# A third factor buffer and packed convolution taps, with the product of delta and x on GpSimd and that of x and D on ScalarE

## The chip, the cores and the metric

The kernel runs on one core of a Trainium2 chip. The time is that of the whole launch in microseconds of the device, as the median of several runs. The profile is of one further execution, whose own time is given beside its span (the time from its first to its last instruction). Engines are named as in the profile: PE (matmuls), DVE (VectorE), ACT (ScalarE), POOL (GpSimd), SP (the queue that issues the DMAs).

## What is computed

Two stages over x of shape (2, 2048, 512), with a residual after each. The first, in which all edits lie, is a small gated recurrence of 64 channels, whose result y0 is expanded to 512 by Wo, and then a Mamba block on it. Cut to what matters:

```python
# recurrence of 64 channels ("cond"): y0 = c_t * state;  h = y0 @ Wo + bo
xn = layernorm(h) * ln_g + ln_b
x_br, z = split(xn @ W_in, 2)                  # 1024 channels each
xb = silu(causal_conv4(x_br, conv_w) + conv_b) # depthwise, 4 taps
Bm, Cm = xb @ W_b, xb @ W_c                    # 16 states
delta = softplus(xb @ W_delta + b_delta)
A_bar = exp(delta[..., None] * A)              # (time, channel, state)
Bx = delta[..., None] * Bm[:, :, None, :] * xb[..., None]
h_t = A_bar_t * h_(t-1) + Bx_t                 # scan over time
y = sum_state(h * Cm) + xb * Dp
x = x + ((y * silu(z)) @ W_out + h)
# second stage: low-rank layer and a feed-forward with weights cut to -1, 0, 1 and activations to 8 bits
```

## The kernel before

All arithmetic of the first stage is in fp32. Time is cut into 16 blocks of T = 256 steps (8 of each of the two sequences, in turn). Channels lie on the 128 partitions, in ND = 8 tiles `dt`; the 16 states are cut into NG = 4 groups of G = 4. A step of the inner loop is a pair (tile, group), q = 0 to NQ - 1 = 31, and every engine walks through the same 32 of them in each block, in an order written out by hand:

- ACT makes the factors A_bar of a group: 4 exponentials of 128x255 from `delta` (line 702), written to one of two PSUM buffers `a_ps` of 4 banks in all. It may start on a buffer once the scan two groups back is through (line 699).
- DVE makes Bx of the next group, one 128x1024 instruction that multiplies u = delta * x (held over the 4 states) by `Bbc`, the broadcast rows of B in SBUF (line 856, `bx`); it writes into a slot of the SBUF `ring` of four. Then it scans the present group (line 864, `scans`), in place in the ring, with the factors as first input and the ring slot as second. Column 0 of each state carries the state over from the last block, so that one scan covers four states.
- For every second tile DVE first makes u for a pair of tiles, from `delta` and `xb`, both in SBUF, into the PSUM bank `u_ps` (line 835).
- POOL copies the last column of the states (line 465) and multiplies the ring slot by `Cbc` in two halves of 128x512 (line 472), both in SBUF. Once for each tile it makes `xdp` = x * D, 128x256 (line 459).
- PE turns and sums the products in the bank `yT_ps` (line 1069, `turn_states`), with `xdp` as first term (line 1063). A ring slot is free for line 856 once its turns are done.
- DVE gates the turned sum with silu(z) (line 799).

Between these steps each engine does the work of the next block (`front`) and what is left of the last (`back`): projections, the small recurrence, the convolution as matmuls, silu, B and C, delta in two halves (the softplus ends on POOL, line 423), and the product with W_out. `plan`, `next_plan` and `back_plan` say at which q. The banks `work[0]` and `work[1]` are handed out in a fixed order of jobs (`BANK`, `jobs_before`). The convolution and its projection are one product: `Mx` holds four matrices of 66 rows (64 channels, one for the bias, one for ln_b), one for each tap, and `x` (lines 1000 to 1011) sums four matmuls of the shifted rows `y0s`. `y0back` (line 535) fills `y0s` on ACT. PSUM is full: 4 banks of factors, 2 of work, one each for `yT_ps` and `u_ps`.

`big[0]`, 128 x 8192 fp32 in SBUF, holds W_in at first, then Mx, Mz, Wcen, the kept y0 and small pieces; in the last block SP fills it with the first feed-forward weights in eight pieces of 1024 columns (lines 306 to 311), among stores of small rows. The second stage waits for all eight (line 1236).

```python
dve.tensor_tensor(u_ps[:, :, 1:T], delta[:, par, dt:dt + 2, 1:T], xb[:, par, dt:dt + 2, 1:T], ALU.mult)
dve.tensor_tensor(ring[:, q % RING, :, :], u_ps[:, dt % 2:dt % 2 + 1, :].to_broadcast([P, G, T]),
                  Bbc[:, G * g:G * g + G, :], ALU.mult)
```

## Time and profile before

| | |
|---|---|
| Time, median of 3 runs | 2658.17 us (2652.7 to 2659.58) |
| Profiled execution: its time and its span | 2653.91 us, 2651.9 us |
| Busy over the span: PE, DVE, ACT, POOL | 2309.5, 2265.5, 1669.0, 1728.4 us |
| Mean granted clock of PE | 0.95 of full speed |
| Line 472 on POOL, Cbc products | 1283.1 us in 1024 |
| Line 864 on DVE, scans | 1168.0 us in 512 |
| Line 856 on DVE, B times u | 619.7 us in 512 |
| Line 702 on ACT, factors | 852.9 us in 2048 |

Busy time is the time in which an engine has an instruction of the program in work; "idle before" is what it stood still ahead of a group, put down to the engine that released it last. In the profile an instruction counts as busy from its start on also while it is held up inside the engine.

### The profile page before, as it was taken

The numbers are of one execution on the slowest core, as the hardware profiler recorded it, in microseconds if no ns is written. First come the engines' busy times: TensorE is split into PE (matmuls) and PEld (weight loads), VectorE is DVE, ScalarE is ACT, GpSimd is POOL, SyncE is SP. The second block draws the span as 40 slices with busy tenths as digits, with TensorE's granted clock in tenths as the row PEclk, the third lists the DMA queues.
The fourth block names the chain that finished last, engine by engine and source line by source line (L and its number), as shares of the span: only waits on it lengthen the run. The fifth ranks groups of instructions, "written<-read, shape, count | busy, mean of one in ns | idle before, by whom it ended". The sixth has DMA issues, their size and how long they took to land. (4 is left out here: it accounts for less than half of the span.)

```text
span 2651.9 us, 34212 instructions
## 1 busy us (share of the span) xinstructions
PE 2309.5 (87%) x11520; PEld 1586.2 (60%) x11520; DVE 2265.5 (85%) x2232; ACT 1669.0 (63%) x3332; POOL 1728.4 (65%) x2042
## 2 busy tenths in 40 slices
PE   7778889888898988888988888888888875999997
PEld 5566667676666666757666666666666322444443
DVE  2399999999999999899999999999999835888886
ACT  2567676667667676767676767676766534555554
POOL 0278787878787878778787778787878711222221
PEclk8889999999999999999999999999998987999999
DMA  4102020202010110102020202020104621111110
GB/s 186 72 1 72 9 76 6 76 5 80 16 65 21 61 53 28 65 17 73 9 72 10 72 10 72 10 76 5 72 10 189 233 83 56 60 64 66 59 52 24
DMA packets 48299, 151.74 MB, mean 57 GB/s; under 512 B 8069, under 2 KB 8965, under 8 KB 45198
## 3 DMA queue, kind: packets, MB, share of 16 engines
q1 hardware_dynamic: 48142, 149.76, 15.9%
q8 instruction: 84, 1.38, 0.2%
q14 instruction: 73, 0.60, 0.1%
HBM read 132.37 MB, written 17.37 MB: 56 GB/s over the span
## 5 line engine op out<-in xcount | busy, mean ns | idle before, releaser
L472 POOL TENSOR_TENSOR ring<-ring,Cbc 128x512 f32<-128x512 f32 x1024 | 1283.1, 1275 | 44.5 <-POOL carry L465 0.4
L864 DVE TENSOR_TENSOR_SCAN ring<-a_ps,ring 128x1024 f32<-128x1024 f32 x512 | 1168.0, 2281 | 106.7 <-ACT a_ps L702 105.2
L702 ACT ACTIVATE a_ps<-delta,nA 128x255 f32<-128x255 f32 x2048 | 852.9, 468 | 380.3 <-DVE ring L864 379.4
L1069 PE MATMUL yT_ps<-ident,ring 128*128 128x128 f32 x4096 | 588.1, 284 | 163.5 <-POOL ring L472 160.0
L1069 PEld LDWEIGHTS yT_ps<-ident,ring 128*128 128x128 f32 x4096 | 475.0, 145 | 282.2 <-POOL ring L472 241.9
L856 DVE TENSOR_TENSOR ring<-u_ps,Bbc 128x1024 f32<-128x1024 f32 x512 | 619.7, 1210 | 16.0 <-PE yT_ps L1069 9.3
L1035 PE MATMUL work<-xb,big 128*128 128x256 f32 x2048 | 476.8, 385 | 10.1 <-ACT zs L560 10.1
L1035 PEld LDWEIGHTS work<-xb,big 128*128 128x128 f32 x2048 | 385.5, 193 | 79.5 <-issue 16.9
L465 POOL TENSOR_TENSOR carry<-ring,half 128x4 f32<-128x4 f32 x512 | 127.1, 248 | 361.2 <-DVE ring L864 359.7
L1051 PE MATMUL work<-Wout,xb 128*128 128x512 f32 x512 | 237.7, 599 | 0.0
L1414 POOL TENSOR_TENSOR m<-m,pows 128x1 f32<-128x1 f32 x64 | 34.2, 549 | 311.4 <-DVE m L1546 311.4
L1008 PE MATMUL work<-y0s,big 128*128 128x256 f32 x1024 | 234.7, 380 | 0.7 <-issue 0.7
L1008 PEld LDWEIGHTS work<-y0s,big 128*128 128x128 f32 x1024 | 188.6, 190 | 24.6 <-issue 1.0
L1051 PEld LDWEIGHTS work<-Wout,xb 128*128 128x128 f32 x512 | 98.1, 196 | 116.4 <-issue 116.4
L1481 PE MATMUL o_ps<-q,qhT 128*128 128x512 bf16 x512 | 119.3, 387 | 11.8 <-DVE qhT L1579 11.8
L1445 PE MATMUL x_ps<-lay,x2T 128*128 128x512 f32 x256 | 122.0, 621 | 0.7 <-ACT x2T L1506 0.7
L567 ACT ACTIVATE xb<-work,V 128x256 f32<-128x256 f32 x128 | 53.5, 469 | 103.7 <-PE work L1008 103.7
L1460 PE MATMUL h_ps<-q,qaT 128*128 128x512 bf16 x512 | 115.7, 379 | 0.0
L423 POOL TENSOR_TENSOR delta<-delta,lnbuf 128x1024 f32<-128x1024 f32 x32 | 75.6, 2363 | 58.8 <-ACT lnbuf L616 58.8
L1024 PE MATMUL work<-xb,Wbc 128*32 128x256 f32 x256 | 77.4, 471 | 33.1 <-ACT xb L576 33.1
L1512 ACT ACTIVATE hb<-hb 128x2048 f32<-128x2048 f32 x32 | 61.2, 1912 | 65.7 <-DVE hb L1565 65.7
L1565 DVE SCALAR_TENSOR_TENSOR hb<-h_ps,m,b1r 128x2048 f32<-128x2048 f32 x32 | 75.2, 2350 | 27.8 <-PE h_ps L1460 27.8
(197 smaller groups left out, 2508.1 us busy)
## 6 DMA issues: line engine op xcount, KB each, us to landing
Bbc<-bc_rows SPq DMA_DIRECT2D x64, 512.0 KB, 4.6
Cbc<-bc_rows SPq DMA_DIRECT2D x64, 512.0 KB, 3.7
xT<-in_xT SPq DMA_DIRECT2D x16, 514.0 KB, 3.5
x_rows<-x2row SPq DMA_DIRECT2D x32, 256.0 KB, 2.0
xp<-x_rows SPq DMA_DIRECT2D x32, 256.0 KB, 2.7
xx<-in_x SPq DMA_DIRECT2D x32, 256.0 KB, 3.0
out_rows<-orow SPq DMA_DIRECT2D x32, 256.0 KB, 2.0
delta<-in_c_w SPq DMA_DIRECT2D x6, 1024.0 KB, 5.3
```

The costliest lines, as they stand in the source:

```text
L465: nc.gpsimd.tensor_tensor(carry[:, par, dt, G * g:G * g + G].rearrange("p (g o) -> p g o", o=1), h[:, :, T - 1:T], ident1, ALU.mult).then_ ...
L472: nc.gpsimd.tensor_tensor(hp, hp, Cbc[:, G * g + GP * c:G * g + GP * c + GP, :], ALU.mult)\
L702: r = nc.scalar.activation(a_ps[q % 2][:, i, 1:T], delta[:, par, dt, 1:T], ACT.Exp, scale=nA[:, dt, s:s + 1])
L856: dve.tensor_tensor(ring[:, q % RING, :, :], u_ps[:, dt % 2:dt % 2 + 1, :].to_broadcast([P, G, T]), Bbc[:, G * g:G * g + G, :], ALU.mult). ...
L864: dve.tensor_tensor_scan(ring[:, q % RING, :, :].rearrange("p g t -> p (g t)"), a_ps[q % 2][:, :, :].rearrange("p g t -> p (g t)"), ring[: ...
L1008: r = pe.matmul(ps[:, T * m:T * m + T], Mx[:, tap, c:c + P], y0s[:, fp, tap:tap + T], start=(tap == 0), stop=(tap == 3))
L1035: r = pe.matmul(ps[:, T * m:T * m + T], Wd[:, d, c:c + P], xb[:, fp, d, :], start=(d == 0), stop=(d == ND - 1))
L1051: r = pe.matmul(ps[:, :], xb[:, fp, d, P * tt:P * tt + P], Wout[:, d, :], start=False, stop=(d == ND - 1))
L1069: r = pe.matmul(yT_ps[:, tt, :], ring[:, q % RING, i, P * tt:P * tt + P], ident[:, :], is_transpose=True, start=False, stop=(g == NG - 1 a ...
L1445: r = pe.matmul(x3_ps[:, :], x2T[:, d, :], lay[:, batch, d, :], start=(d == 0), stop=(d == KD - 1))
L1460: r = pe.matmul(h_ps[:, 512 * c:512 * c + 512], qaT[:, d, :], q1[:, d, 512 * c:512 * c + 512], start=(d == 0), stop=(d == KD - 1))
L1481: r = pe.matmul(o_ps[:, :], qhT[:, d, :], q2[:, d, :], start=(d == 0), stop=(d == KF - 1))
```

## The change

- A third factor buffer `a_sb` in SBUF (in `big[0]`); group number n of the whole run uses buffer n mod 3, on ACT and on DVE, and ACT may be three groups ahead.
- u is made by POOL (`inputs`), a pair of tiles ahead, into two buffers in `big[0]` (SBUF); the bank `u_ps` is given up. DVE's line 856 waits for POOL's product and reads u from there.
- `xdp` is made by ACT (`skip`) and no more by POOL.
- Taps: the rows for taps 0 and 1 of the 64 channels are packed one above the other into one matrix of 128 rows, read against `yp`, that ACT copies together from `y0s`; the two further rows of taps 0 and 1 go to partitions 96 and 97 of the matrices for taps 2 and 3, and `y0s` has shifted copies there. So 3 matmuls of 128 rows stand for 4 of 66. ACT makes three more small copies a block. The setup is changed to match.
- The pieces of `big[0]` that hold these buffers till later (3, 7 and 6) are loaded later: piece 3 once line 856 has come to its last 8 groups, piece 7 after its last, piece 6 after the last scan.

The diff, without the declarations and the setup of Mx:

```diff
...
-        Mx = big[0][:, 0:4 * DI].rearrange("p (k c) -> p k c", k=4)
+        Mx = big[0][:, 0:3 * DI].rearrange("p (k c) -> p k c", k=3)
+        yp = big[0][:, 3 * DI:3 * DI + T]
         Mz = big[0][:, 4 * DI:5 * DI]
-        y0k = big[0][:, 6 * DI:6 * DI + 2 * T].rearrange("p (b t) -> p b t", b=2)
+        y0k = big[0][:, 5 * DI + D:6 * DI].rearrange("p (b t) -> p b t", b=2)
+        a_sb = big[0][:, 6 * DI:7 * DI].rearrange("p (g t) -> p g t", g=G)
...
+        a_of = [a_ps[0], a_ps[1], a_sb]
+        NA = len(a_of)
         abank = [a_ps[i // 2][:, 2 * (i % 2):2 * (i % 2) + 2, :].rearrange("p a b -> p (a b)") for i in range(4)]
-        u_full = pb("u_ps", [P, 512])
-        u_ps = u_full[:, :].rearrange("p (m t) -> p m t", m=2)
+        u_of = [big[0][:, c:c + 2 * T].rearrange("p (m t) -> p m t", m=2) for c in (3 * DI + T, 7 * DI + D)]
...
-                        if 2 <= c < 9:
+                        if 2 <= c < 8 and c != 5:
                             sp.dma_start(big[0][:, DI * (c - 2):DI * (c - 1)], f_w1[:, DI * (c - 2):DI * (c - 1)])\
                                 .then_inc(s_big[0], 16)
-                    sp.wait_ge(s_col0, NCOL * NBLK)
+                    sp.wait_ge(s_bx, NQ * NBLK - 8)
+                    sp.dma_start(big[0][:, 3 * DI:4 * DI], f_w1[:, 3 * DI:4 * DI]).then_inc(s_big[0], 16)
+                    sp.wait_ge(s_bx, NQ * NBLK)
                     sp.dma_start(big[0][:, 7 * DI:8 * DI], f_w1[:, 7 * DI:8 * DI]).then_inc(s_big[0], 16)
+                    sp.wait_ge(s_scan, NQ * NBLK)
+                    sp.dma_start(big[0][:, 6 * DI:7 * DI], f_w1[:, 6 * DI:7 * DI]).then_inc(s_big[0], 16)
...
+            def inputs(b, bp, j):
+                pool.wait_ge(s_delta, 2 * b + j // 2 + 1)
+                pool.wait_ge(s_xb, 2 * b + j // 2 + 1)
+                wait(pool, s_bx, NQ * b + 8 * (j - 1))
+                nc.gpsimd.tensor_tensor(u_of[j % 2][:, :, 1:T], delta[:, bp, 2 * j:2 * j + 2, 1:T],
+                                        xb[:, bp, 2 * j:2 * j + 2, 1:T], ALU.mult).then_inc(s_u, 1)
             def step(k, par, front, back, scan):
                 for q in range(NQ):
                     dt, g = q // NG, q % NG
+                    if front and q == SUMS[0] + 1:
+                        if isinstance(k, int) and k == -1:
+                            pool.wait_ge(s_mz, 2)
+                        inputs(k + 1, 1 - par, 0)
+                    if scan and q in (3, 11, 19):
+                        inputs(k, par, (q + 5) // 8)
...
-                    if g == 0:
-
-                        wait(pool, s_xb, 2 * k + (2 if dt >= ND // 2 else 1))
-                        wait(pool, s_tr, NQ * k + NG * (dt - 2) + 1)
-                        nc.gpsimd.tensor_tensor(xdp[:, dt % 2, :], xb[:, par, dt, :],
-                                                V[:, V_DP + dt:V_DP + dt + 1].to_broadcast([P, T]), ALU.mult)\
-                            .then_inc(s_xdp, 1)
-
...
-                    act.wait_ge(s_yh, n + 1)
-                    nc.scalar.activation(y0s[0:NY, fp, 3:T + 3], ps[0:NY, 0:T], ACT.Copy).then_inc(free[BANK["YB"]], 1)
+                    act.wait_ge(s_yh, 2 * n + 1)
+                    nc.scalar.activation(y0s[0:NY, fp, 3:T + 3], ps[0:NY, 0:T], ACT.Copy).then_inc(s_yh, 1)
+                    act.wait_ge(s_yh, 2 * n + 2)
+                    nc.scalar.activation(yp[0:N0, :], y0s[0:N0, fp, 0:T], ACT.Copy)
+                    nc.scalar.activation(yp[N0:2 * N0, :], y0s[0:N0, fp, 1:T + 1], ACT.Copy)
+                    nc.scalar.activation(y0s[CROW:CROW + 2, fp, 2:T + 3], y0s[N0:NY, fp, 0:T + 1], ACT.Copy)\
+                        .then_inc(free[BANK["YB"]], 1)
...
+                def skip(b, bp, dt):
+                    wait(act, s_xb, 2 * b + (2 if dt >= ND // 2 else 1))
+                    wait(act, s_tr, NQ * b + NG * (dt - 2) + 1)
+                    nc.scalar.activation(xdp[:, dt % 2, :], xb[:, bp, dt, :], ACT.Copy, scale=V[:, V_DP + dt:V_DP + dt + 1])\
+                        .then_inc(s_xdp, 1)
...
+                    if scan and g == 3 and dt < ND - 1:
+                        skip(k, par, dt + 1)
+                    if front and q == NQ - 3:
+                        skip(n, fp, 0)
...
-                    wait(act, s_scan, NQ * k + q - 1)
+                        act.wait_ge(s_aclr, 5)
+                    wait(act, s_scan, NQ * k + q - NA + 1)
                     for i in range(G):
                         s = G * g + i
-                        r = nc.scalar.activation(a_ps[q % 2][:, i, 1:T], delta[:, par, dt, 1:T], ACT.Exp,
+                        r = nc.scalar.activation(a_of[(NQ * k + q) % NA][:, i, 1:T], delta[:, par, dt, 1:T], ACT.Exp,
...
                 def mx_scale():
+                    dve.wait_ge(s_mtz, 1)
                     for m in range(ND):
                         if m % 4 == 0:
                             dve.wait_ge(s_mxt, m // 4 + 1)
                         ps = abank[m // 4][:, NY * (m % 4):NY * (m % 4) + NY]
-                        for tap in range(4):
-                            r = dve.tensor_scalar(MTk[:, m, tap, :], ps, V[:, V_CW + 4 * m + tap:V_CW + 4 * m + tap + 1],
-                                                  None, ALU.mult)
+                        cw = [V[:, V_CW + 4 * m + tap:V_CW + 4 * m + tap + 1] for tap in range(4)]
+                        for tap in range(2):
+                            dve.tensor_scalar(MTk[:, m, 0, N0 * tap:N0 * tap + N0], ps[:, 0:N0], cw[tap], None, ALU.mult)
+                            dve.tensor_scalar(MTk[:, m, 1 + tap, CROW:CROW + 2], ps[:, N0:NY], cw[tap], None, ALU.mult)
+                            r = dve.tensor_scalar(MTk[:, m, 1 + tap, 0:NY], ps, cw[2 + tap], None, ALU.mult)
                         r.then_inc(s_mxs, 1)
...
-                        delta_ready(dve, k, dt)
-                        dve.wait_ge(s_xb, 2 * k + (2 if dt >= ND // 2 else 1))
-                        wait(dve, s_bx, NQ * k + q)
-                        dve.tensor_tensor(u_ps[:, :, 1:T], delta[:, par, dt:dt + 2, 1:T], xb[:, par, dt:dt + 2, 1:T],
-                                          ALU.mult).then_inc(s_u, 1)
                         if isinstance(k, int) and k == 0:
-                            dve.wait_ge(s_aclr, 1)
+                            dve.wait_ge(s_aclr, 2)
                         dve.wait_ge(s_u, ND // 2 * k + dt // 2 + 1)
...
                     dve.tensor_tensor(ring[:, q % RING, :, :],
-                                      u_ps[:, dt % 2:dt % 2 + 1, :].to_broadcast([P, G, T]),
+                                      u_of[dt // 2 % 2][:, dt % 2:dt % 2 + 1, :].to_broadcast([P, G, T]),
                                       Bbc[:, G * g:G * g + G, :], ALU.mult).then_inc(s_bx, 1)
...
                     dve.tensor_tensor_scan(ring[:, q % RING, :, :].rearrange("p g t -> p (g t)"),
-                                           a_ps[q % 2][:, :, :].rearrange("p g t -> p (g t)"),
+                                           a_of[(NQ * k + q) % NA][:, :, :].rearrange("p g t -> p (g t)"),
                                            ring[:, q % RING, :, :].rearrange("p g t -> p (g t)"), 0.0,
                                            ALU.mult, ALU.add).then_inc(s_scan, 1)
...
-                    for tap in range(4):
-                        r = pe.matmul(ps[:, T * m:T * m + T], Mx[:, tap, c:c + P], y0s[:, fp, tap:tap + T],
-                                      start=(tap == 0), stop=(tap == 3))
+                    for i, rows in enumerate((yp[:, :], y0s[:, fp, 2:T + 2], y0s[:, fp, 3:T + 3])):
+                        r = pe.matmul(ps[:, T * m:T * m + T], Mx[:, i, c:c + P], rows, start=(i == 0), stop=(i == 2))
...
```

## Rows read from the trace of the kernel before

**Rows 1.** Stretches, three of sixteen blocks: us, then busy time by engine, clock, DMA.

```profile
core 0: us, PE busy (x) PEld busy (x) DVE busy (x) ACT busy (x) POOL busy (x), PEclk, DMA share, GB/s
97.90:234.00 136.10, 111.16 (x560) 88.66 (x560) 115.79 (x94) 92.01 (x200) 97.17 (x120) 0.89 0.06 20
...
1242.90:1369.10 126.20, 111.97 (x573) 83.78 (x572) 117.96 (x96) 85.72 (x190) 100.51 (x119) 0.96 0.12 43
...
2000.30:2130.00 129.70, 115.01 (x508) 58.84 (x506) 120.02 (x97) 71.73 (x160) 98.90 (x115) 0.95 0.60 222
```

**Rows 2.** Waits of the whole run: us in total, times, longest.

```profile
ACT a_ps L702 <- DVE ring L864: 379.4, 300, 4.1
POOL carry L465 <- DVE ring L864: 359.7, 323, 5.3
...
DVE ring L864 <- ACT a_ps L702: 105.2, 63, 4.6
...
DVE ring L856 <- PE yT_ps L1069: 9.3, 17, 2.9
```

**Rows 3.** Groups by line: busy us, mean ns of one, idle before.

```profile
L472 POOL TENSOR_TENSOR ring<-ring,Cbc 128x512 f32<-128x512 f32 x1024 | 1283.1, 1275 | 44.5 <-POOL carry L465 0.4
L864 DVE TENSOR_TENSOR_SCAN ring<-a_ps,ring 128x1024 f32<-128x1024 f32 x512 | 1168.0, 2281 | 106.7 <-ACT a_ps L702 105.2
...
L856 DVE TENSOR_TENSOR ring<-u_ps,Bbc 128x1024 f32<-128x1024 f32 x512 | 619.7, 1210 | 16.0 <-PE yT_ps L1069 9.3
...
L1008 PE MATMUL work<-y0s,big 128*128 128x256 f32 x1024 | 234.7, 380 | 0.7 <-issue 0.7
...
L459 POOL TENSOR_TENSOR xdp<-xb,V 128x256 f32<-128x256 f32 x128 | 79.1, 618 | 0.1
...
L835 DVE TENSOR_TENSOR u_ps<-delta,xb 128x510 f32<-128x510 f32 x64 | 58.3, 911 | 46.6 <-POOL delta L423 46.6
L567 ACT ACTIVATE xb<-work,V 128x256 f32<-128x256 f32 x128 | 53.5, 469 | 103.7 <-PE work L1008 103.7
...
L540 ACT ACTIVATE y0s<-work 66x256 f32<-66x256 f32 x16 | 6.1, 382 | 0.5
```

**Rows 4.** Lines one by one: durations in ns min/median/max, first and last start.

```profile
L835 DVE TENSOR_TENSOR u_ps<-delta,xb x64: 666/675/1774, 98.0 to 2096.6; 128x510 f32<-128x510 f32 x64
...
L472 POOL TENSOR_TENSOR ring<-ring,Cbc x1024: 1255/1274/1782, 105.5 to 2131.9; 128x512 f32<-128x512 f32 x171
...
L465 POOL TENSOR_TENSOR carry<-ring,half x512: 192/202/659, 105.2 to 2130.4; 128x4 f32<-128x4 f32 x171
...
L864 DVE TENSOR_TENSOR_SCAN ring<-a_ps,ring x512: 2266/2280/2292, 102.8 to 2127.5; 128x1024 f32<-128x1024 f32 x171
...
L856 DVE TENSOR_TENSOR ring<-u_ps,Bbc x512: 1191/1202/1226, 100.4 to 2124.1; 128x1024 f32<-128x1024 f32 x171
```

**Rows 5.** Timeline at 1242 us: start, duration, engine, line.

```profile
1242.53 2.50 POOL L472 TENSOR_TENSOR ring<-ring,Cbc 128x512 f32<-128x512 f32 x2
...
1243.82 1.77 DVE L835 TENSOR_TENSOR u_ps<-delta,xb 128x510 f32<-128x510 f32 x1
...
1244.99 0.64 POOL L465 TENSOR_TENSOR carry<-ring,half 128x4 f32<-128x4 f32 x1
```

**Rows 6.** Timeline at 1210 us, the same product with POOL idle.

```profile
1210.16 0.68 DVE L835 TENSOR_TENSOR u_ps<-delta,xb 128x510 f32<-128x510 f32 x1
1210.33 0.56 POOL L465 TENSOR_TENSOR carry<-ring,half 128x4 f32<-128x4 f32 x1 [0.52 <-DVE ring L864]
```

**Rows 7.** Timeline at 739 us, the product started ahead of POOL's second.

```profile
738.88 2.95 POOL L472 TENSOR_TENSOR ring<-ring,Cbc 128x512 f32<-128x512 f32 x2
...
740.03 0.67 DVE L835 TENSOR_TENSOR u_ps<-delta,xb 128x510 f32<-128x510 f32 x1
```

**Rows 8.** DMA issues: KB each, median us to landing.

```profile
big<-in_f_w SPq DMA_DIRECT2D x8, 512.0 KB, 6.4
```

**Rows 9.** The reading of the feed-forward weights, line 1237.

```profile
L1237 ACT ACTIVATE q<-big x2: 7015/7024/7032, 2162.2 to 2169.3; 128x8192 bf16<-128x8192 f32 x2
```

More of the change, by code:

```diff
@@ L33 @@
 NY = N0 + 2
+CROW = 96
 EPS = 1e-5
@@ L156, in scan_phase @@
         WoTg = xdp[:, :, :].rearrange("p a b -> p (a b)")[:, 0:KD * NY].rearrange("p (d n) -> p d n", d=KD)
-        MTk = ring[:, 1:RING, :, :].rearrange("p a b c -> p (a b c)")[:, 0:ND * 4 * NY]\
-            .rearrange("p (m k n) -> p m k n", m=ND, k=4)
+        MTk = ring[:, 1:RING, :, :].rearrange("p a b c -> p (a b c)")[:, 0:ND * 3 * P]\
+            .rearrange("p (m k n) -> p m k n", m=ND, k=3)
         cond = V[:, V_COND:V_COND + 2 * KD].rearrange("p (d b) -> p d b", b=2)
@@ L194, in scan_phase @@
         s_mxs = sem("s_mxs")
+        s_mtz = sem("s_mtz")
         s_mxp = sem("s_mxp")
@@ L550, in mx_copy @@
                         act.wait_ge(s_mxp, m + 1)
-                        nc.scalar.activation(Mx[0:NY, :, P * m:P * m + P],
-                                             abank[2 + m % 2][0:NY, :].rearrange("p (k c) -> p k c", k=4), ACT.Copy)\
+                        nc.scalar.activation(Mx[:, :, P * m:P * m + P],
+                                             abank[2 + m % 2][:, 0:3 * P].rearrange("p (k c) -> p k c", k=3), ACT.Copy)\
                             .then_inc(s_mxc, 1)
@@ L697, in step @@
                         act.wait_ge(s_setD, 8)
-                        act.wait_ge(s_aclr, 3)
-                    wait(act, s_scan, NQ * k + q - 1)
+                        act.wait_ge(s_aclr, 5)
+                    wait(act, s_scan, NQ * k + q - NA + 1)
                     for i in range(G):
                         s = G * g + i
-                        r = nc.scalar.activation(a_ps[q % 2][:, i, 1:T], delta[:, par, dt, 1:T], ACT.Exp,
+                        r = nc.scalar.activation(a_of[(NQ * k + q) % NA][:, i, 1:T], delta[:, par, dt, 1:T], ACT.Exp,
                                                  scale=nA[:, dt, s:s + 1])
@@ L723, in _ @@
             dve.tensor_scalar(nA[:, :, :], nA[:, :, :], -1.0, None, ALU.mult).then_inc(s_setD, 1)
+            dve.memset(MTk[:, :, 1:3, NY:P], 0.0).then_inc(s_mtz, 1)
             dve.wait_ge(s_w[0], 16)
@@ L850, in bx @@
                     elif g == 0:
-                        if dt % 2:
-                            dve.wait_ge(s_bx, NQ * k + q)
+                        dve.wait_ge(s_bx, NQ * k + q)
                         dve.tensor_reduce(Bbc[:, :, 0], first[:, dt, :].rearrange("p (s o) -> p s o", o=1), AX.X, ALU.add)\
@@ L877, in step @@
                             .then_inc(s_wcen, 1)
-                        dve.memset(u_ps[:, :, 0:1], 1.0).then_inc(s_aclr, 1)
+                        for i in range(2):
+                            dve.memset(u_of[i][:, :, 0:1], 1.0).then_inc(s_aclr, 1)
+                        dve.memset(a_sb[:, :, 0:1], 0.0).then_inc(s_aclr, 1)
                         dve.wait_ge(s_mxc, ND)
@@ L995, in turn_m @@
                             pe.wait_ge(s_mxc, m - 1)
-                        for tap in range(4):
-                            r = pe.transpose(abank[2 + m % 2][0:NY, P * tap:P * tap + P], MTk[:, m, tap, :], ident[:, :])
+                        for i in range(3):
+                            r = pe.transpose(abank[2 + m % 2][:, P * i:P * i + P], MTk[:, m, i, :], ident[:, :])
                         r.then_inc(s_mxp, 1)
@@ L1006, in x @@
                     c = P * (2 * j + m)
-                    for tap in range(4):
-                        r = pe.matmul(ps[:, T * m:T * m + T], Mx[:, tap, c:c + P], y0s[:, fp, tap:tap + T],
-                                      start=(tap == 0), stop=(tap == 3))
+                    for i, rows in enumerate((yp[:, :], y0s[:, fp, 2:T + 2], y0s[:, fp, 3:T + 3])):
+                        r = pe.matmul(ps[:, T * m:T * m + T], Mx[:, i, c:c + P], rows, start=(i == 0), stop=(i == 2))
                     if m:
@@ L1015, in z @@
                     tt, c = j // 2, 512 * (j % 2)
-                    pe.matmul(ps[:, :], y0s[:, fp, 3 + P * tt:3 + P * tt + P], Mz[:, c:c + 512],
+                    pe.matmul(ps[:, :], y0s[0:NY, fp, 3 + P * tt:3 + P * tt + P], Mz[0:NY, c:c + 512],
                               start=True, stop=True).then_inc(full[BANK[f"Z{j}"]], 1)
```

## The prediction

> **What bounds the kernel now.** I read the page first for busy shares and slices, then the stretches of one block each, then the waits, then the durations of the groups. The scan phase runs from 98 to about 2130 us; the rest is the feed-forward phase, which no edit reaches except through three loads. The phase is periodic: a block takes 126.2 us, in which DVE is busy 118.0, PE 111.9, POOL 100.5 and ACT 85.7 [rows 1]. DVE is the bound: it is idle for 8.2 us a block, and most of that is the scan waiting for ACT's factors, 105.2 us in 63 waits, 6.6 a block [rows 2]. ACT may run only two groups ahead, and what else it has to do between two groups comes through to DVE. ACT and POOL wait for the scan far more than it waits for them [rows 2], so they have room: 40 and 26 us a block.
>
> Then I asked why the product of delta and x on DVE has a mean of 911 ns and a median of 675 [rows 3, 4]. The timeline answers. At 1243.82 the product starts while POOL's pair of Cbc products, begun at 1242.53, still runs; it takes 1.77 us and ends at 1245.59, 0.56 after POOL's pair has ended at 1245.03 [rows 5]. At 1210.16 POOL is idle as it starts; now it takes 0.68, and POOL's small copy, begun 0.17 later, takes 0.56 in place of its usual 0.20 and ends just after it [rows 4, 6]. At 740.03 the product starts a little before POOL's second Cbc product: it takes 0.67, and POOL's pair 2.95 in place of 2.50 [rows 5, 7]. So these two engines exclude each other for a whole instruction, whoever came first going first. The product is the one frequent DVE instruction here whose two inputs both lie in SBUF. The B-times-u product (line 856) takes u from PSUM, the scan (864) its factors from PSUM, and both keep to their durations beside a POOL that is busy four fifths of the time: 1191 to 1226 and 2266 to 2292 ns [rows 3, 4]. The two PSUM operands keep DVE and POOL apart.
>
> **What the change does to this.** It moves u to SBUF, and with it every one of the 512 instructions of line 856 gets two SBUF inputs; and it puts the third factor buffer in SBUF, so that every third scan does too. The exclusion now concerns 64 short products; it will concern 512 + 171 long instructions, against a POOL that all the while multiplies by Cbc from SBUF.
>
> The Trainium skill has the same thing as a rule: "SBUF — State Buffer", section "Who interferes with whom", says that a DVE instruction with two SBUF inputs contends with a GpSimd instruction that reads SBUF, that the one issued first has the shared port pair for the whole instruction, and that the other blocks fully. By that rule this trace agrees (1.77 for 0.68 us). The page does not name the scan; with the rule applied to it the sum is the one below, without it that of the second rival.
>
> **The sum, per block.** What must be laid end to end is POOL's own work plus what DVE holds POOL out.
> - POOL now: 100.5 [rows 1]. Less 8 products of x and D at 0.618: 4.9. Plus 4 products of delta and x; the nearest row is the Cbc product, 512 elements with two SBUF inputs, 1283.1 / 1024 = 1.25 each: 5.0 [rows 3]. Less what DVE's old product cost it, three times 0.36 and once 0.45 a block, 1.5 [rows 4, 6, 7]. Together 99.1.
> - Each exclusive instruction of DVE: of one that waited, 0.56 of 0.68 came after POOL's end, so 0.12 of it is hidden behind POOL. The small copy behind it ended 0.44 late where DVE needed 0.56 [rows 5], so POOL hides 0.12 too. An exclusive instruction costs POOL its duration less 0.24.
> - Line 856: 32 x (1.20 - 0.24) = 30.7. Scans on the SBUF buffer: 171 / 16 = 10.7 a block x (2.28 - 0.24) = 21.8. The durations are those of PSUM operands [rows 3, 4]; the product with SBUF alone, 675 ns for 510 elements, lies on the same line (1202 - 675 = 527 ns for 514 more), so I don't change them.
> - 99.1 + 30.7 + 21.8 = 151.6.
>
> Does DVE come out longer? Its own work is 118.0 - 58.3 / 16 = 114.3 [rows 1, 3]. A scan on SBUF stands right behind line 856 and right ahead of the next, so one POOL instruction slips in on each side: 10.7 x 2 x (1.25 - 0.12) = 24. The other 21.3 of line 856 meet POOL at a random place, some 0.5 each: 11. That is 149, a little less: POOL ends last, but closely, so the ring of four states won't always keep POOL fed. For that idle time I add an estimate of 3 (between 0 and the 8.2 that the bound engine is idle today). 154.6 a block, 28.4 more than 126.2; over 16 blocks (the first and last are about as long as the others [rows 1]) 454 us. The profiled execution took 2653.9 us for a span of 2651.9, and the median of the runs is 2658.2, 4 us above; on 2654 the sum gives **3108 us**.
>
> Bounds of this case: without idle time 151.6, so 3060; with both engines' full durations and nothing hidden, 99.1 + 38.4 + 24.3 = 161.8, so 3224.
>
> **The parts that cost nothing**, and what covers them:
> - *Products of x and D on ACT*: 8 a block at about 0.47, that of a 128x256 copy of line 567 [rows 3], 3.8 us, in ACT's idle 40 us. ACT issues the product for a tile ahead of waiting factors, and the state that it waits for was turned a tile before. Without the cover: 3.8 x 16 = 60 us.
> - *Third factor buffer*: worth at most the 6.6 us a block of waits for factors, 105 us in all, if DVE stayed the bound. Here it is not: DVE waits for POOL instead, ACT is early anyway, and the gain is nothing.
> - *u made by POOL ahead*: takes 3.6 us a block from DVE (58.3 in all) and adds the 5.0 counted above. Queued behind it on POOL are the copy of the states and the Cbc products; behind these PE's turns and so DVE's next line 856. The wait of POOL on delta and x is met long before; the one on line 856 eight groups back too. At a block's start DVE waits for a product that POOL issues three groups ahead of the end.
> - *Packed taps*: 3 matmuls in place of 4, a quarter of the 234.7 us of PE in line 1008, 3.7 a block [rows 3]. PE is at 112 of 126 now and would be at 108 of 155. Three more small ACT copies (0.38 each, row of line 540 [rows 3]) lie ahead of the first of them and hold up PE's queue by some 1.1 us a block, 18 in all if nothing covered it; PE's 46 idle us do.
> - *Loads of the feed-forward weights*: pieces 3, 7 and 6 now wait on SP for DVE's last instructions, and three small row stores stand behind them. The last piece starts at the end of the last scan, about 2130 us on the old scale, lands 6.4 us later, and is read at 2162 [rows 4, 8, 9]. Hidden; without it 6 us once.
> - *Setup* ahead of the first block: 48 smaller DVE multiplications for 32, 24 turns for 32, and one memset. A few us of either sign, once.
>
> **Rivals.**
> 1. *The exclusion does not touch line 856 or the scan* (a held broadcast, or a scan that reads at half pace, might leave POOL room). Then DVE falls to 114.3 and, with two thirds of the factor waits gone, idles some 2: 116.3, 9.9 less a block, 158 in all: **2496 us**. Against it: the row of line 835 is the same operation on the same engine; only held u and the output's place differ. It decides if line 856 keeps 1.20 us beside a busy POOL. 5 in 100.
> 2. *Only line 856 excludes, the scan doesn't*: 99.1 + 30.7 + 3 = 132.8, 6.6 more, **2760 us**. For it: no row shows a scan with two SBUF inputs, and it takes an element in two of the product's times. 10 in 100.
> 3. *The exclusion costs more than the hidden 0.24 allows*: each hand-over at full price and DVE and POOL both starving each other through the ring. 161.8 + 3 = 164.8, **3272 us**. 7 in 100.
> 4. *Gains and losses cancel within 0.3%*: needs an exclusion of a tenth of the size seen. 1 in 100.
>
> The forecast's own case has 77 in 100, and 3050 to 3230 around it. The range from 2740 to 3240 leaves out rivals 1 and 3 and the lower half of 2. A difference under 0.3% can't be told from no change; faster 0.05, same 0.01, slower 0.94.
>
> **What would show it.** Right: line 856 with a mean far over 1.20 us, split between about 1.2 and 2.3; a third of the scans well above 2.28, the others at it; the Cbc product with a mean over 1.6 for 1.27; POOL's share of the scan phase near 100% by the profile's count; waits of the scan for factors almost gone, those of line 856 for PE's turns (9.3 us now [rows 2]) grown to hundreds; a block of about 155 us. Wrong: line 856 at 1.20 flat (rival 1), or all scans at 2.28 (rival 2). The mechanism would also be mis-sized if DVE could take the port twice in a row, past a waiting POOL.

## The result: 3143.7 us, 18% slower

The changed kernel takes 3143.72 us (median of 4 runs, 3142.34 to 3147.95) against 2656.8 for the kernel before in the same series: a ratio of 1.1837, 95% interval 1.1816 to 1.1858. The prediction was 3108, with 2740 to 3240 as range. The profiled execution has a span of 3140.8 us, 488.9 more than before.

First the stretches of one block each, from line 886 to line 886, for the changed kernel; the columns are those of [rows 1], and the last row sums fifteen stretches, from the first block to the fifteenth.

```profile
core 0: us, PE busy (x) PEld busy (x) DVE busy (x) ACT busy (x) POOL busy (x), PEclk, DMA share, GB/s
99.00:258.50 159.50, 116.63 (x553) 89.35 (x551) 128.19 (x91) 95.32 (x209) 132.21 (x109) 0.83 0.05 17
258.50:418.70 160.20, 122.86 (x558) 89.68 (x557) 131.85 (x92) 89.36 (x200) 148.34 (x114) 0.85 0.10 34
418.70:577.30 158.60, 123.32 (x555) 89.62 (x554) 134.17 (x92) 89.39 (x200) 148.43 (x116) 0.85 0.12 40
577.30:729.70 152.40, 118.97 (x562) 86.87 (x561) 132.86 (x92) 89.08 (x200) 145.00 (x113) 0.88 0.09 29
...
sum 2362.50, PE 1822.83 PEld 1335.06 DVE 1992.36 ACT 1345.09 POOL 2195.78; mean PE 121.52 PEld 89.00 DVE 132.82 ACT 89.67 POOL 146.39
```

Without the first stretch that is 157.4 us a block ((2362.50 - 159.50) / 14), with POOL busy 147.4 and DVE 133.2 of them by the same division. Before it was 126.2, 100.5 and 118.0 [rows 1]. Fourteen blocks of 31.2 us more are 437 of the 489 us; the rest lies in the first and the last block. POOL is now the busiest engine, and the pattern of three block lengths (160, 158.5, 152.4) comes from the third buffer, which falls on other groups in each of three blocks: with the third buffer alone (e2 below) the pattern is there too, with two buffers (e3) it is not.

Then the groups by line, to be read against [rows 3]. Line 886 is what 856 was, 894 was 864, 487 was 472, 480 was 465 and 1040 was 1008; 439 makes u on POOL, and 655 makes x times D on ACT.

```profile
L487 POOL TENSOR_TENSOR ring<-ring,Cbc 128x512 f32<-128x512 f32 x1024 | 1643.1, 1625 | 44.2
...
L886 DVE TENSOR_TENSOR ring<-big,Bbc 128x1024 f32<-128x1024 f32 x512 | 803.3, 1569 | 29.9 <-PE yT_ps L1100 21.5
L894 DVE TENSOR_TENSOR_SCAN ring<-a_ps,ring 128x1024 f32<-128x1024 f32 x342 | 779.2, 2279 | 29.7 <-ACT a_ps L734 29.3
...
L894 DVE TENSOR_TENSOR_SCAN ring<-big,ring 128x1024 f32<-128x1024 f32 x170 | 474.7, 2792 | 39.1 <-ACT big L734 39.1
L480 POOL TENSOR_TENSOR carry<-ring,half 128x4 f32<-128x4 f32 x512 | 338.3, 661 | 125.0 <-DVE ring L894 125.0
...
L439 POOL TENSOR_TENSOR big<-delta,xb 128x510 f32<-128x510 f32 x64 | 123.1, 1924 | 0.0
...
L655 ACT ACTIVATE xdp<-xb,V 128x256 f32<-128x256 f32 x128 | 64.8, 506 | 0.4
L835 DVE TENSOR_TENSOR gbuf<-yT_ps,zs 128x256 f32<-128x256 f32 x128 | 54.0, 422 | 221.3 <-PE yT_ps L1100 218.8
```

The reader sees one line split in two. The 342 scans whose factors are in PSUM (`ring<-a_ps,ring`) take 2279 ns, as before. The 170 whose factors are in SBUF (`ring<-big,ring`) take 2792. Line 886 rose from 1210 to 1569, the Cbc product from 1275 to 1625, and the copy of four columns from 248 to 661.

The durations one by one (ns, min/median/max) show that this is no slower instruction: the fastest are as fast as ever [rows 4], and the slowest are longer by up to about one of the other engine's long instructions: the 3316 ns of line 886 stood behind the last step of the softplus on POOL (line 432), the 3359 ns of line 487 behind a scan.

```profile
L886 DVE TENSOR_TENSOR ring<-big,Bbc x512: 1191/1425/3316, 99.1 to 2613.4; 128x1024 f32<-128x1024 f32 x171
...
L894 DVE TENSOR_TENSOR_SCAN ring<-big,ring x170: 2272/2565/4103, 116.6 to 2610.2; 128x1024 f32<-128x1024 f32 x170
...
L487 POOL TENSOR_TENSOR ring<-ring,Cbc x1024: 1259/1271/3359, 104.3 to 2622.4; 128x512 f32<-128x512 f32 x171
...
L480 POOL TENSOR_TENSOR carry<-ring,half x512: 191/204/2181, 103.9 to 2620.9; 128x4 f32<-128x4 f32 x171
```

One passage of the timeline, DVE's rows and then POOL's:

```profile
1498.46 2.28 DVE L894 TENSOR_TENSOR_SCAN ring<-big,ring 128x1024 f32<-128x1024 f32 x1
1500.67 2.22 DVE L886 TENSOR_TENSOR ring<-big,Bbc 128x1024 f32<-128x1024 f32 x1
1505.22 0.43 DVE L835 TENSOR_TENSOR gbuf<-yT_ps,zs 128x256 f32<-128x256 f32 x1 [2.33 <-PE yT_ps L1100]
...
1498.68 5.33 POOL L487 TENSOR_TENSOR ring<-ring,Cbc 128x512 f32<-128x512 f32 x2
```

The scan has both inputs in SBUF and was first. POOL's pair, 0.22 us later, stands until it ends at 1500.74. By the durations the first of the pair runs then, and line 886, started at 1500.67, stands: 2.22 us for 1.20. Its end frees the second of the pair. Over five us went for two POOL instructions that need 2.50, and after it DVE is idle for 2.33, ahead of the gate, for PE's turns, which wait for POOL's late pair.

Last, what DVE waits for in the changed kernel (us in total, times, longest), against [rows 2]:

```profile
DVE gbuf L835 <- PE yT_ps L1100: 218.8, 76, 4.5
...
DVE Bbc L883 <- PE yT_ps L1100: 57.8, 54, 3.8
DVE ring L894 <- ACT big L734: 39.1, 21, 4.2
...
DVE ring L894 <- ACT a_ps L734: 29.3, 17, 3.6
...
DVE ring L886 <- PE yT_ps L1100: 21.5, 28, 2.7
```

The waits for factors fell from 105.2 to 68.4; those for PE's turns, that is mostly for POOL ahead of PE, are 298, where before they were 22.3 (9.3 at line 856 [rows 2], 8.8 at line 853 and 4.2 at the gate).

### The profile page after: what moved, and what is told of

The parts are those of the page before. It is cut to its first block and busy times, and to the rows that moved or that the text cites. A ratio compares the mean times of both kernels' runs of the same rounds, so it can differ in the third digit from the quotient of the medians.

```text
span 3140.8 us, 33737 instructions
## 1 busy us (share of the span) xinstructions
PE 2461.6 (78%) x11224; PEld 1663.1 (53%) x11256; DVE 2508.6 (80%) x2187; ACT 1725.3 (55%) x3508; POOL 2459.5 (78%) x1978
## 3 DMA queue, kind: packets, MB, share of 16 engines
q8 instruction: 81, 1.33, 0.2%
## 5 line engine op out<-in xcount | busy, mean ns | idle before, releaser
L487 POOL TENSOR_TENSOR ring<-ring,Cbc 128x512 f32<-128x512 f32 x1024 | 1643.1, 1625 | 44.2
L1100 PE MATMUL yT_ps<-ident,ring 128*128 128x128 f32 x4096 | 681.0, 307 | 539.6 <-POOL ring L487 533.5
L886 DVE TENSOR_TENSOR ring<-big,Bbc 128x1024 f32<-128x1024 f32 x512 | 803.3, 1569 | 29.9 <-PE yT_ps L1100 21.5
L894 DVE TENSOR_TENSOR_SCAN ring<-a_ps,ring 128x1024 f32<-128x1024 f32 x342 | 779.2, 2279 | 29.7 <-ACT a_ps L734 29.3
L734 ACT ACTIVATE a_ps<-delta,nA 128x255 f32<-128x255 f32 x1368 | 567.0, 469 | 46.2 <-DVE ring L894 45.6
L894 DVE TENSOR_TENSOR_SCAN ring<-big,ring 128x1024 f32<-128x1024 f32 x170 | 474.7, 2792 | 39.1 <-ACT big L734 39.1
L480 POOL TENSOR_TENSOR carry<-ring,half 128x4 f32<-128x4 f32 x512 | 338.3, 661 | 125.0 <-DVE ring L894 125.0
L734 ACT ACTIVATE big<-delta,nA 128x255 f32<-128x255 f32 x680 | 288.5, 501 | 30.6 <-DVE ring L894 30.3
L835 DVE TENSOR_TENSOR gbuf<-yT_ps,zs 128x256 f32<-128x256 f32 x128 | 54.0, 422 | 221.3 <-PE yT_ps L1100 218.8
L1040 PE MATMUL work<-y0s,big 128*128 128x256 f32 x512 | 146.5, 412 | 0.0
L1512 PE MATMUL o_ps<-q,qhT 128*128 128x512 bf16 x481 | 111.6, 385 | 18.8 <-DVE qhT L1610 18.6
L439 POOL TENSOR_TENSOR big<-delta,xb 128x510 f32<-128x510 f32 x64 | 123.1, 1924 | 0.0
```

The costliest lines, as they stand in the source:

```text
L439: nc.gpsimd.tensor_tensor(u_of[j % 2][:, :, 1:T], delta[:, bp, 2 * j:2 * j + 2, 1:T], xb[:, bp, 2 * j:2 * j + 2, 1:T], ALU.mult).then_inc( ...
L480: nc.gpsimd.tensor_tensor(carry[:, par, dt, G * g:G * g + G].rearrange("p (g o) -> p g o", o=1), h[:, :, T - 1:T], ident1, ALU.mult).then_ ...
L487: nc.gpsimd.tensor_tensor(hp, hp, Cbc[:, G * g + GP * c:G * g + GP * c + GP, :], ALU.mult)\
L734: r = nc.scalar.activation(a_of[(NQ * k + q) % NA][:, i, 1:T], delta[:, par, dt, 1:T], ACT.Exp, scale=nA[:, dt, s:s + 1])
L886: dve.tensor_tensor(ring[:, q % RING, :, :], u_of[dt // 2 % 2][:, dt % 2:dt % 2 + 1, :].to_broadcast([P, G, T]), Bbc[:, G * g:G * g + G, : ...
L894: dve.tensor_tensor_scan(ring[:, q % RING, :, :].rearrange("p g t -> p (g t)"), a_of[(NQ * k + q) % NA][:, :, :].rearrange("p g t -> p (g ...
```

## The experiments

**e1: u in SBUF and nothing else** (kernel before; DVE still makes it).

```diff
-        u_full = pb("u_ps", [P, 512])
-        u_ps = u_full[:, :].rearrange("p (m t) -> p m t", m=2)
+        u_ps = big[0][:, 7 * DI + D:8 * DI].rearrange("p (m t) -> p m t", m=2)
...
-                    sp.wait_ge(s_col0, NCOL * NBLK)
+                    sp.wait_ge(s_bx, NQ * NBLK)
```

> The kernel before with one tensor moved: u lies in SBUF (in big[0]) instead of its PSUM bank, still made by DVE, still one buffer. Theory 1, DVE and POOL exclude each other when a DVE instruction has two SBUF inputs: POOL's 100.5 us a block plus 32 x 0.9 to 0.96 held out gives 129 to 131, with 3 to 8 idle 132 to 139 a block, so 2750 to 2860 us; line 856 has a mean of 1.5 us or more and POOL's Cbc product one of 1.45 or more; scans stay at 2.28. Rival, the loss of the changed kernel comes from DVE waiting for a product that now stands in POOL's queue: nothing changes here, 2655 us, 1.20 us for line 856.

**e2: the third buffer in SBUF and nothing else** (kernel before; `y0k` moves to make room, and the piece under the buffer is loaded after the last scan). ACT and DVE both take buffer n mod 3, as in the change.

```diff
+        a_sb = big[0][:, 6 * DI:7 * DI].rearrange("p (g t) -> p g t", g=G)
...
+        a_of = [a_ps[0], a_ps[1], a_sb]
...
-                    wait(act, s_scan, NQ * k + q - 1)
+                    wait(act, s_scan, NQ * k + q - NA + 1)
```

> The kernel before with the third factor buffer in SBUF alone, so that 171 of the 512 scans have two SBUF inputs; u stays in PSUM. Theory 1: POOL's 100.5 + 10.7 x 2.04 = 122 is still below the block of 126, so most of the exclusion is hidden in POOL's idle 26 us; DVE's own third scans wait some 0.5 us each (5 a block) and the waits for factors (6.6) shrink to about 2, so 124 to 129 a block, 2620 to 2700 us; scans on the SBUF buffer at 2.6 to 2.9 us mean. Rival, a scan does not exclude POOL: 2.28 us for all scans, the factor waits go, 2560 to 2590 us.

**e3 and e4: one of the two undone in the changed kernel.** In e3 `a_of` has two buffers; in e4 `u_ps` is again a PSUM bank that DVE fills, and POOL's `inputs` is gone.

```diff
-        a_of = [a_ps[0], a_ps[1], a_sb]
+        a_of = [a_ps[0], a_ps[1]]
```

> The changed kernel without its third factor buffer: two PSUM buffers, all scans with one PSUM input; u in SBUF made by POOL, packed taps and the product of x and D on ACT stay. Theory 1: POOL's 99 + 30 = 129, with 3 to 8 idle 132 to 137 a block, 2750 to 2830 us: about two thirds of the loss goes although only a quarter of the exclusive instructions do, because what is left fits better under POOL's idle time. Rival, the loss is that of DVE waiting for POOL's u: stays above 3050 us.

> The changed kernel with u back in its PSUM bank, made by DVE; third buffer in SBUF, packed taps and the product of x and D on ACT stay. Theory 1: as the third buffer alone, and POOL has 4.9 us less to do: 123 to 128 a block, 2600 to 2690 us. Rival, the scans on the SBUF buffer are the larger part of the loss (2.78 us mean, 10.7 a block, and all that waits behind them): above 2800 us.

| | median us | ratio to before (95%) | more than before |
|---|---|---|---|
| e1, u in SBUF | 2902.39 | 1.0937 (1.0918 to 1.0955) | 248 |
| e2, third buffer in SBUF | 2807.59 | 1.0582 (1.0565 to 1.0600) | 154 |
| e3, changed, two buffers | 2865.18 | 1.0803 (1.0785 to 1.0821) | 211 |
| e4, changed, u in PSUM | 2782.59 | 1.0488 (1.0470 to 1.0505) | 129 |

In e1 one tensor in another memory costs 9.4%. Two groups of it:

```profile
L863 DVE TENSOR_TENSOR_SCAN ring<-a_ps,ring 128x1024 f32<-128x1024 f32 x512 | 1166.6, 2279 | 125.2 <-ACT a_ps L701 123.8
L855 DVE TENSOR_TENSOR ring<-big,Bbc 128x1024 f32<-128x1024 f32 x512 | 812.2, 1586 | 10.4 <-PE yT_ps L1068 3.7
```

All scans are at 2279 and only the product with u in SBUF is at 1586: the exclusion goes with the operand. In e2 it is the other way round, the product at 1209 and the 170 scans on SBUF at 2676:

```profile
L861 DVE TENSOR_TENSOR ring<-u_ps,Bbc 128x1024 f32<-128x1024 f32 x512 | 619.1, 1209 | 24.6 <-PE yT_ps L1075 17.5
L869 DVE TENSOR_TENSOR_SCAN ring<-big,ring 128x1024 f32<-128x1024 f32 x170 | 454.9, 2676 | 52.2 <-ACT big L707 51.6
```

So the scan excludes too, which no row of before could show, and the rival that blames the order (DVE behind POOL's u) is out: in e1 DVE makes u itself.

All four lie above the ranges that I had expected, e1 and e3 by about 40 us, e2 and e4 by about 100. The mechanism was right, and for u in SBUF POOL's sum was too: in the blocks behind the first POOL is busy 131.0 us of 141.7 in e1 and 129.2 of 139.9 in e3, where I had 129 to 131 and 129. What was too small is POOL's idle time, 10.6 and 10.7 us for 3 to 8.

```profile
99.50:248.40 148.90, 115.03 (x563) 89.84 (x562) 128.92 (x95) 91.56 (x200) 123.13 (x113) 0.88 0.06 19
...
sum 2132.00, PE 1762.14 PEld 1319.83 DVE 1978.91 ACT 1288.88 POOL 1957.16; mean PE 117.48 PEld 87.99 DVE 131.93 ACT 85.93 POOL 130.48
```

DVE's side adds up too. DVE also stands for the other engine, and it was the bound: in e1 it is busy 132.1 us a block for 118.0, of which 512 x (1.586 - 1.210) = 193 us of the run lie in line 855 alone, and it keeps its old idle time; the factor waits didn't shrink (123.8 for 105.2). In e2 DVE's own extra time came out as expected (busy 123.4, 5.4 more), and POOL is busy only 117.1 of a block of 135.7. But the waits for factors stayed at 103.4 us of the run (51.8 + 51.6), where I had put 2 a block, and those for PE's turns grew from 22.3 to 90.8. POOL's idle time did not swallow what DVE stood. The two single losses, 248 and 154, add up to 402 of the 487.

**e5 and e7: both operands back in PSUM.** e5 is the changed kernel with two PSUM factor buffers and u by DVE in PSUM, so that only the packed taps and the product of x and D on ACT are left. e7 has the packed taps alone, with the product back on POOL:

```diff
+                    if g == 0:
...
+                        nc.gpsimd.tensor_tensor(xdp[:, dt % 2, :], xb[:, par, dt, :],
+                                                V[:, V_DP + dt:V_DP + dt + 1].to_broadcast([P, T]), ALU.mult)\
+                            .then_inc(s_xdp, 1)
...
-                    if scan and g == 3 and dt < ND - 1:
-                        skip(k, par, dt + 1)
-                    if front and q == NQ - 3:
-                        skip(n, fp, 0)
```

> The changed kernel with both SBUF operands undone: two factor buffers in PSUM, u made by DVE into its PSUM bank; left are the packed taps and the product of x and D on ACT. Both of my theories say that these two cost nothing and bring little, since DVE stays the bound: 2640 to 2665 us, line 856's successor at 1.21 us, scans at 2.28. Rival: three more copies and eight products on ACT make the factors later, 3 to 5 us a block of more waits, 2700 us or more.

> The kernel before with the packed taps alone (3 matmuls of 128 rows for 4 of 66, and three more ACT copies); x times D on POOL, two PSUM factor buffers, u on DVE in PSUM. The run with taps and the product of x and D moved took 2618.6 us, 40 us less than before, where I had expected nothing. Theory, PE's front work is on the path to ACT's factors (ACT stands in order behind jobs of PE): the taps carry most of it, 2618 to 2635 us. Rival, it is POOL's 4.9 us a block less that count (POOL finishes states earlier, so PE's turns and DVE's u product collide less): the taps alone stay at 2645 to 2660.

e5: 2618.6 us, 0.9840 (0.9824 to 0.9857). e7: 2620.12 us, 0.9848 (0.9835 to 0.9862). Both are faster than before, by 1.5 to 1.6%, and the taps carry all of it. DVE's and ACT's waits in e7 show where:

```profile
DVE ring L891 <- ACT a_ps L725: 66.1, 63, 4.4
...
ACT xb L583 <- PE work L1035: 57.1, 49, 3.0
```

ACT stood 103.7 us for PE's convolution product before, by the group of line 567 [rows 3], and stands 57.1 now; behind it on ACT come silu and the next factors, and DVE's wait for factors falls from 105.2 [rows 2] to 66.1. That is 39 us for the 40 gained; that the one follows from the other is read from ACT's order and these waits, no run isolates it. The product of x and D on ACT is an exchange more than nothing: from e7 to e5 DVE's waits for factors grow from 66.1 to 78.3 us, and its busy time falls from 2269.0 to 2254.3, mostly by its product of delta and x (703 ns for 911), which now meets POOL less often.

With e5 as base the sum of the two operands is plainer: u in SBUF and made by POOL costs 247 (e3), the third buffer alone 164 (e4), both together 525. Together they cost more than one by one. (The kernel before itself differed by up to 6 us between the series of these runs.)

**e6: POOL's instructions made short**, all SBUF placements kept. The kernel leaves out the product with C for 255 of 256 columns, so its result is not the reference's.

```diff
-                        nc.gpsimd.tensor_tensor(hp, hp, Cbc[:, G * g + GP * c:G * g + GP * c + GP, :], ALU.mult)\
+                        nc.gpsimd.tensor_tensor(hp[:, :, 0:1], hp[:, :, 0:1], Cbc[:, G * g + GP * c:G * g + GP * c + GP, 0:1], ALU.mult)\
```

> The changed kernel, whose POOL multiplies only the first of 256 columns of each state by C, so the result is not the reference's: POOL's 64 instructions of 1.27 us a block become 64 short ones, and all placements in SBUF stay. Theory 1, exclusion: the SBUF operands cost nothing by themselves, so line 886 falls to 1.20 to 1.27 us and the scans on the SBUF buffer to 2.28 to 2.4, a block takes 117 to 121 us, and the launch 2500 to 2590 us, less than before. Rival, an SBUF operand makes DVE's instruction itself longer, or the lower clock of TensorE is what costs: the two keep their 1.57 and 2.79 us, and the time stays above 2900.

```profile
L894 DVE TENSOR_TENSOR_SCAN ring<-a_ps,ring 128x1024 f32<-128x1024 f32 x342 | 779.7, 2280 | 44.3 <-ACT a_ps L734 43.5
L886 DVE TENSOR_TENSOR ring<-big,Bbc 128x1024 f32<-128x1024 f32 x512 | 647.3, 1264 | 29.7 <-PE yT_ps L1100 22.6
...
L894 DVE TENSOR_TENSOR_SCAN ring<-big,ring 128x1024 f32<-128x1024 f32 x170 | 389.0, 2288 | 46.8 <-ACT big L734 46.2
```

1264 and 2288 ns: the SBUF operands cost next to nothing by themselves (the median of line 886 is 1216 for 1202), and the loss against the kernel before is gone (2652.43 us, one run); against e5, which has the taps too, 34 us are left. But the time is not the 2500 to 2590 that I expected. DVE still waits 89.7 us for factors and 72 for turns, at the ring and at the gate, with three buffers and a light POOL. That was a first sign that the third buffer is worth less than DVE's waits for factors say.

**w1: the operands the other way round**, built on the changed kernel. All three factor buffers lie in SBUF and line 856's result in PSUM, so that a scan has one input in each; DVE makes u in PSUM again, the ring has three slots, and packed taps and x times D on ACT stay.

```diff
-RING = 4
+RING = 3
...
+        a_of = [big[0][:, 4 * DI:5 * DI].rearrange("p (g t) -> p g t", g=G),
+                big[0][:, 6 * DI:7 * DI].rearrange("p (g t) -> p g t", g=G), sb("a_sb", [P, G, T])]
...
-                    wait(dve, s_tr, NQ * k + q + 1 - RING)
...
-                    dve.tensor_tensor(ring[:, q % RING, :, :],
+                    wait(dve, s_scan, NQ * k + q - 1)
+                    dve.tensor_tensor(bx_ps[q % 2][:, :, :],
...
-                    dve.tensor_tensor_scan(ring[:, q % RING, :, :].rearrange("p g t -> p (g t)"),
+                    wait(dve, s_tr, NQ * k + q + 1 - RING)
+                    dve.tensor_tensor_scan(ring[:, (NQ * k + q) % RING, :, :].rearrange("p g t -> p (g t)"),
...
-                                           ring[:, q % RING, :, :].rearrange("p g t -> p (g t)"), 0.0,
+                                           bx_ps[q % 2][:, :, :].rearrange("p g t -> p (g t)"), 0.0,
```

> The operands the other way round: all three factor buffers in SBUF, and line 856's result in two PSUM buffers, so that a scan has one input in each and writes the ring (three slots, claimed at the scan); u by DVE in PSUM, packed taps and x times D on ACT. No frequent DVE instruction has two SBUF inputs. A wait on the scan before the last now stands ahead of each line 856, which ends the overlap of 0.08 us between a scan and its successor, up to 2.7 a block. Theory 1: durations 1.21 and 2.28 flat, waits for factors from 6.6 to 1 or 2 a block, so 121 to 124 a block, 2575 to 2625 us. Rival, the third buffer does not bring the waits down, because ACT is late for another reason: 126 to 129 a block, 2655 to 2700 us.

**w2: w1 with ACT's jobs one step later** from z's first copy on.

```diff
+                else:
+                    next_plan = {q + (q > 20): jobs for q, jobs in next_plan.items()}
```

> The kernel with factors in SBUF and Bx in PSUM, and ACT's jobs for the next block from z's first copy on put one step later in its order, since with a third buffer ACT comes to them one group earlier and stands there for PE (4.4 and 6.2 us in one block, ahead of z's copies). Theory: of the 2.8 us a block that scans 27, 30 and 31 still wait for factors most goes: 120.5 to 122 a block, 2565 to 2595 us. Rival, the waits there are of ACT's own load at the block's end: unchanged, 2600 to 2615, or longer if delta comes later.

w1: 2610.52 us, 0.9816 (0.9799 to 0.9832). w2: 2604.77 us, 0.9794 (0.9781 to 0.9807), the fastest of all. Scans and products in w2:

```profile
L889 DVE TENSOR_TENSOR_SCAN ring<-big,bx_ps 128x1024 f32<-128x1024 f32 x342 | 778.7, 2277 | 32.2 <-ACT big L722 29.3 <-PE yT_ps L1093 2.9
L880 DVE TENSOR_TENSOR bx_ps<-u_ps,Bbc 128x1024 f32<-128x1024 f32 x512 | 630.7, 1232 | 17.3
L889 DVE TENSOR_TENSOR_SCAN ring<-a_sb,bx_ps 128x1024 f32<-128x1024 f32 x170 | 387.1, 2277 | 15.0 <-ACT a_sb L722 15.0
```

Factors in SBUF and no exclusion: the scans' means are 2277, beside a POOL that is busy 95.9 of 122.7 us in a block. The waits for factors are 62.0 in w1 (41.1 + 20.9) and 44.3 in w2 (29.3 + 15.0), for 78.3 in e5. In w1 that is 3.9 us a block, where I had expected 1 or 2. ACT, now further ahead, stands for PE ahead of z's copies, in the order that was written out for two buffers: 175.1 us in w1, 79.5 in w2, and 73.7 in e5:

```profile
ACT zs L567 <- PE work L1038: 175.1, 39, 6.2
```

Moving the jobs took most of that stand out of ACT and 18 us out of DVE's waits for factors, but only 6 us out of the time: 2604.8 lies in the range of the rival, not in the 2565 to 2595 that I expected. Against e5, w2 is 14 us faster. DVE's waits for factors are 34 us less (44.3 for 78.3), far from the 105 that three buffers could at most have saved, and 28 of the 34 are spent again: DVE is busy 2282.3 us for 2254.3. Line 880 takes 1232 ns for 1210, 11 us in all, and it no longer overlaps the scan ahead of it, for which it now waits; how much is due to its output in PSUM and how much to the wait was not separated.

**e8: the gate one step later** in the changed kernel.

```diff
-                    if back and q == 1:
+                    if back and q == 2:
...
-                    if scan and q % NG == 1 and q > 1:
+                    if scan and q % NG == 2 and q > 2:
```

> The changed kernel with DVE's gate of a tile one step later in DVE's order (after line 886 of two groups ahead instead of one), nothing else. In the changed kernel DVE stands 13.8 us a block ahead of the gate for the last turns of its tile, a stricter wait than the ring's four slots, and while it stands POOL runs out of scanned states (10.0 us idle a block). Theory, this order is what keeps the block above the 151.6 that POOL's sum gives: 150 to 155 a block, 3030 to 3110 us. Rival, the wait only moves on, to the ring or to PE, whose turns of the next tile wait for the gate: 3130 us or more.

3122.83 us, 1.1744 (1.1726 to 1.1761) to before, some 21 us less than the changed kernel. The waits of DVE:

```profile
DVE Bbc L883 <- issue: 70.8, 31, 4.8
...
DVE ring L886 <- PE yT_ps L1100: 64.2, 52, 3.8
DVE ring L894 <- ACT big L734: 59.8, 21, 6.2
DVE Bbc L883 <- PE yT_ps L1100: 50.8, 30, 3.6
```

The gate's 218.8 us are gone but for 5.3, but the lines at the ring wait 115 for 79, line 883 stands another 70.8 us for which the profile names no releaser, the scans wait 103 for 68, and the instructions themselves stand longer (means of 1608 ns for line 886 and 2939 for the scans on SBUF, for 1569 and 2792). The time lies between my two expectations, nearer the rival. In the blocks behind the first POOL is busy 146.1 us of 156.2, so it is still idle for 10.1: the order of the gate is not what keeps the block above POOL's sum.

## Why the prediction held, step by step

- **The mechanism**: as predicted, shown by e1 and e2 (the durations go with the operand), by e6 (they go back when POOL's instructions are short) and by w1 and w2 (SBUF factors are free if the other input is in PSUM).
- **It touches the scan**: argued from the rule of the Trainium skill ("SBUF — State Buffer", section "Who interferes with whom") and from the likeness to the product, shown by e2. Rivals 1 and 2 are out; rival 3 too, for POOL was held out less than my sum has it, not more (next point).
- **POOL's sum, 151.6**: measured 147.4. POOL's own work was put at 99.1, so DVE held it out for 48.3 and not 52.5; over 42.7 exclusive instructions that is 1.13 us for one, where I had 1.23. Some of DVE's instructions found POOL idle: by the trace 74 of the 598 exclusive ones in these fourteen blocks started so, and an instruction of POOL that comes later stands only for what is left.
- **The idle time, 3**: measured 10.0 (157.4 - 147.4). This is the term that was mis-sized, and it hides that the other was too large; together they gave 154.6 for 157.4, hence 3108 for 3144. I took idle time as a remnant of the ring. That two errors of opposite sign nearly cancel, while the same way of summing missed single operands by up to 108 us, makes the closeness of 3108 in part luck. What makes POOL idle stays open. It is idle for about the same time in e1, e3 and e8 (10.6, 10.7, 10.1), so neither u on POOL, nor the third buffer, nor the gate's place in the order is the cause by itself. My reading of the trace is that POOL's work is bunched at the block's end (delta, first columns), where it falls behind, and that it catches up in the middle and stands again for the scan: it is idle for 3.6% of a block's first quarter and 9% of its middle quarter. That is argued and not shown. A rival that no run separates is PE: it was busy 121.9 of 157.4 us in a block, for 111.9 of 126.2 before, and its mean granted clock was 0.868 of full speed for 0.950, so it ran for more of the time at 1.2 GHz in place of 2.4. PE's turns, through which POOL's product reaches the gate and the ring, took 307 ns each for 284 (line 1100, before 1069), 681.0 us for 588.1, so at most 5.8 us a block.
- **DVE's sum, 149**: it is busy 133.2, that is 18.9 over its own 114.3 where I had put 35; the other 24.2 of the block it is idle, mostly because POOL's states are late (the 298 us of waits for turns are 18.6 a block). The view that one sum ends last was too simple, as the misses of e2 and e4 show, where neither POOL nor DVE is near the block.
- **Parts at nothing**: x times D on ACT, 0.506 us for 0.47, costs nothing in sum (e5 against e7: 1.5 us, within the noise). The loads are hidden: the reading of the weights starts at 2652.8, 191.3 after the last block's start at 2461.5, for 161.9 before [rows 1, 9], and the 29.4 more are no more than a block has. **Packed taps at nothing was wrong**: 40 us of gain. The step that failed is "PE is at 112 of 126": its busy share says nothing of a product that ACT waits for in order. Whether the new bound covers the gain in the changed kernel no run shows; with one operand in SBUF it was not covered: e4 is 25 us below e2, from which it differs by the taps and the product of x and D, and e3, in which POOL also makes u, is 37 below e1.
- **The third buffer at nothing here**: no run shows a gain from it, and with u in SBUF it costs 278 us (changed kernel against e3). But its reason, "ACT is early anyway", was wrong: the scan's waits for factors, which were to be almost gone, are 68.4 us. And without the exclusion the 105 us that I gave as the most it could be worth were far off: in w2 34 of them went, and the launch gained 14 over e5.
- **Where DVE would wait**: for PE's turns, as said, but at the gate (218.8) and hardly at line 886 (21.5). The gate needs the turns of the last group of its tile, sooner than the ring needs a slot. POOL's share of a block is 94%, not quite the "near 100%" of my signs; the other signs came as written (1569 and 2792 ns, the Cbc product at 1625, a block of 157.4).

## What to carry to other kernels

Before moving a tensor from PSUM to SBUF, count which DVE instructions would then have two SBUF inputs, and how busy POOL is meanwhile; swap the homes of two operands rather than put both on one side. Price an exclusion on both engines, each with its present idle time: in e2 POOL was idle for 18.7 us of a block, and it did not pay for what DVE stood. Even where POOL's sum was right, some 10 us a block of idle time came on top. And an engine with time to spare can still be late for an engine that serves its jobs in order; look at the waits for its results, not at its busy share.

## What the chip showed that I had not expected

- A DVE scan with both inputs in SBUF excludes POOL like a product, for its whole 2.28 us, though it takes only 0.45 elements a ns (1024 in 2280 ns) where the product takes 0.85.
- DVE instructions with one SBUF input can stand too. In e1 the copy of y0 (line 778, both ends in SBUF, was 779) has a mean of 1263 ns for 352, and the clip of e0 (line 749, was 750) 656 for 261, where the shifted schedule puts them beside a POOL instruction. At 1439.78 us the copy starts while POOL's pair of Cbc products, begun at 1438.47, runs until 1440.95; it takes 1.33 us and ends at 1441.11:

```profile
L778 DVE COPY big<-y 128x256 f32<-128x256 f32 x16 | 20.2, 1263 | 6.7 <-issue 6.7
L749 DVE TENSOR_SCALAR e<-e 64x256 f32<-64x256 f32 x16 | 10.5, 656 | 9.1 <-ACT e L499 9.1
```

  By "SBUF — State Buffer", section "Who interferes with whom", of the Trainium skill, a copy or a tensor with a scalar in DVE's two-port mode can take the port pair that DVE shares with GpSimd, and the two then exclude each other; this trace agrees, in that both instructions stand.
- ACT's exponential takes 501 ns into SBUF and 469 into PSUM in the changed kernel (line 734), 32 ns more for 255 elements; in w1, where all go to SBUF, it takes 501.

```profile
L734 ACT ACTIVATE a_ps<-delta,nA 128x255 f32<-128x255 f32 x1368 | 567.0, 469 | 46.2 <-DVE ring L894 45.6
L734 ACT ACTIVATE big<-delta,nA 128x255 f32<-128x255 f32 x680 | 288.5, 501 | 30.6 <-DVE ring L894 30.3
```
